# Moving a softmax factor from GpSimd to VectorE, one reciprocal and one product per head

## The reference, cut to what matters

```
q, k, v = x@Wq, x@Wk, x@Wv          # q and k in two halves (q1,q2),(k1,k2), each rotated (rope)
a1 = softmax(q1 k1^T * scale + causal mask);  a2 = softmax(q2 k2^T * scale + causal mask)
lam = exp(sum(lambda_q1*lambda_k1)) - exp(sum(lambda_q2*lambda_k2)) + LAMBDA_INIT
out = (a1 - lam*a2) @ v             # then a norm per head over time, @Wo
x = layernorm(x + attention);  x = layernorm(x + ffn(x))   # silu(up)*gate, ternary weights
```

## Time and profile before

| | us |
|---|---|
| median of 3 runs | 2203.5 (2202.45 to 2203.89) |
| profiled execution, its own time | 2204.31 |
| its span, first to last instruction | 2202.3 |
| TensorE busy in the span | 2124.7 (96%) |
| VectorE busy | 1691.1 (77%) |
| ScalarE busy | 1457.0 (66%) |
| GpSimd busy | 1197.9 (54%) |

### The profile page before, as it was taken

One profiled execution on the slowest core, in us unless ns is written; L12 is line 12 of the kernel. 1 busy time (PEld: TensorE's weight loads), 2 busy tenths in 40 slices (PEclk: granted clock), 3 DMA queues, 4 the chain that ended last, 5 costly groups with the idle time before them and its releaser, 6 DMA issues.

```text
span 2202.3 us, 41179 instructions
## 1 busy us (share of the span) xinstructions
PE 2124.7 (96%) x13314; PEld 1362.0 (62%) x13314; DVE 1691.1 (77%) x3701; ACT 1457.0 (66%) x3450; POOL 1197.9 (54%) x1919
## 2 busy tenths in 40 slices
PE   8999999999999999999999999999999999999998
PEld 4666666666665666666666666666666666654443
DVE  4888787889888878888878888888778888853333
ACT  0777777767777777777767777777677687742232
POOL 0577676677656655555555655655554556541232
PEclk9999999999999999999999999999999999999999
DMA  7766566757656422221453322241543213114000
GB/s 248 202 207 217 194 208 209 239 178 221 191 164 152 136 73 61 89 68 58 150 134 82 94 75 78 91 125 54 166 107 70 71 40 96 40 49 112 4 20 19
DMA packets 291218, 263.85 MB, mean 120 GB/s; under 512 B 65088, under 2 KB 233152, under 8 KB 288960
## 3 DMA queue, kind: packets, MB, share of 16 engines
q1 hardware_dynamic: 246016, 220.26, 33.7%
q10 hardware_dynamic: 44992, 40.98, 6.8%
HBM read 181.48 MB, written 71.30 MB: 115 GB/s over the span
## 4 chain that ended last, share of the span: by engine, by line
PE 76%; DVE 7%; POOL 6%; issue 5%; ACT 4%; DMA 1%; ACTq 1%; DVEq 0%; SPq 0%; POOLq 0%
PE PS L1166 19%; PE PS L1115 10%; PE PS L1096 9%; PE PS L1077 9%; PE PS L1135 9%; PE PS L1175 9%; PE PS L1156 8%; PE PS L1142 2%; POOL linv L1383 2%; DVE e_long L1458 2%; ACT e_long L1227 2%; ACT dt_long L1217 1%; POOL coef L1384 1%; DVE e_long L1524 1%; PE PS L1081 1%
## 5 line engine op out<-in xcount | busy, mean ns | idle before, releaser
L1383 POOL TENSOR_TENSOR linv<-lsum,powers 128x2 f32<-128x2 f32 x512 | 418.3, 817 | 412.5 <-ACT e_long L1227 331.1
L1227 ACT ACTIVATE e_long<-e_long,nmax 128x768 f32<-128x768 f32 (+3 forms) x512 | 504.8, 987 | 150.8 <-DVE nmax L1458 145.1
L1458 DVE CUSTOM_DVE_ANT_0 e_long<-PS,mask_b 128x768 f32<-128x768 f32 (+3 forms) x512 | 516.1, 1019 | 70.6 <-PE PS L1096 49.7
L1096 PE MATMUL PS<-kstk,qstk 128*128 128x384 f32 (+5 forms) x1536 | 470.7, 412 | 27.5 <-DVE nmax L1458 16.8
L1096 PEld LDWEIGHTS PS<-kstk,qstk 128*128 128x128 f32 x1536 | 268.2, 190 | 149.9 <-issue 84.2
L1217 ACT ACTIVATE dt_long<-PS 128x512 f32<-128x512 f32 (+3 forms) x544 | 257.8, 514 | 131.6 <-PE PS L1077 120.8
L1524 DVE SCALAR_TENSOR_TENSOR e_long<-e_long,coef 128x1024 f32<-128x1024 f32 (+3 forms) x256 | 276.3, 1079 | 69.6 <-POOL coef L1384 69.0
L1227 ACT ACTIVATE e_short<-e_short,nmax 128x384 f32<-128x384 f32 (+3 forms) x512 | 283.1, 557 | 17.6 <-DVE nmax L1458 16.8
L1396 POOL TENSOR_TENSOR hid<-th,hid 128x512 f16<-128x512 f32 x128 | 147.9, 1160 | 248.3 <-DVE e_short L1524 124.5
L1077 PE MATMUL PS<-ident,e_long 128*128 128x128 f32 x1664 | 238.8, 275 | 14.8 <-DVE e_long L1524 6.2
L1384 POOL TENSOR_SCALAR coef<-lsum,linv,neglam 128x1 f32<-128x1 f32 x512 | 219.7, 429 | 53.4
(11 more groups left out here) (117 smaller groups left out, 3124.0 us busy)
## 6 DMA issues: line engine op xcount, KB each, us to landing
qstk<-dq SPq DMA_DIRECT2D x512, 128.0 KB, 2.9
dq<-hl SPq DMA_DIRECT2D x25, 1024.0 KB, 5.0
wr<-in_w_proj ACTq DMA_DIRECT2D x48, 512.0 KB, 4.9
kstk<-dk SPq DMA_DIRECT2D x64, 256.0 KB, 5.2
da<-ra SPq DMA_DIRECT2D x32, 512.0 KB, 3.5
at_sb<-da SPq DMA_DIRECT2D x32, 512.0 KB, 4.3
wt<-in_w_up SPq DMA_DIRECT2D x16, 512.0 KB, 6.3
wt<-in_w_gate SPq DMA_DIRECT2D x16, 512.0 KB, 5.4
```

What stands on the lines that cost most here:

```text
L1096: last = nc.tensor.matmul(slot[:, h, :], qstk[:, duo % 4, 2 * r + m, :].bitcast(F32R), kstk[:, g % 2, m, h * w:(h + 1) * w].bitcast(F32R), ...
L1227: nc.scalar.activation(e, e, ACT.Exp, bias=nmax[:, u % 8:u % 8 + 1], scale=-1.0, accum_out=lsum[:, n % 4, m:m + 1]).then_inc(s_exp, 1)
L1383: link(nc.gpsimd.tensor_tensor(linv[:, a % 8, :], lsum[:, a % 4, :], mone, ALU.pow))
L1458: nc.vector.tensor_tensor_reduce(out, slot, mask, -1.0, -NEG, ALU.add, ALU.min, nmax[:, u % 8:u % 8 + 1]).then_inc(s_negmax, 1)
```

## The change: what it does, and the diff

The item "factor" moves from GpSimd's strings to VectorE's. For each head VectorE takes the reciprocal of the second sum (128x1) and then a product of the first sum, that reciprocal and -lambda (128x1), with a link between the two. GpSimd keeps a new item, "inverse", once per duo: a power of -1 on the duo's two first sums (128x2) and the broadcast copy into `wide`. It waits for the exponential of map 0 of the second head only, and is placed before the last `turn` of that head. `lsum` gets 8 places in place of 4, `linv` 4 in place of 8, and `coef` 4 columns in place of 2 (two hold the reciprocals). The planner's cost of "factor" becomes 0.4 in place of 1.15 or 1.4, and "inverse" costs 1.1.

```diff
@@ takes
-    if what == "factor":
-        return 1.4 if STEPS[a].r else 1.15
-            "hidden low": 1.32, "rsqrt": 1.5, ... "group": 1.5, "settle": 1.25, "side": 1.1}
+            "hidden low": 1.32, "rsqrt": 1.5, ... "group": 1.5, "factor": 0.4, "inverse": 1.1, "settle": 1.25, "side": 1.1}
@@ after
     elif what == "turn":
         out = [ITEM("combine", a)]
+        if STEPS[a].r and b == turns(a) - 1:
+            out.append(ITEM("inverse", STEPS[a].duo))
...
     elif what == "factor":
         out = [ITEM("exponent", a, 1), ITEM("minus lambda")]
-        if STEPS[a].r and STEPS[a].duo >= 2:
-            second = heads_of(STEPS[a].duo - 2)[1]
+    elif what == "inverse":
+        out = [ITEM("exponent", heads_of(a)[1], 0)]
+        if a >= 2:
+            second = heads_of(a - 2)[1]
             out.append(ITEM("turn", second, turns(second) - 1))
@@ STRINGS
     "dve": [[ITEM("minimum", n, m) for n, m in _maps],
-            [ITEM("combine", n) for n in _heads], [ITEM("product", duo) for duo in range(DUOS)],
+            [ITEM("factor", n) for n in _heads], [ITEM("combine", n) for n in _heads], [ITEM("product", duo) for duo in range(DUOS)],
...
-    "pool": [[ITEM("factor", n) for n in _heads], [ITEM("hidden low", j) for j in OF_KIND["gate"]],
+    "pool": [[ITEM("inverse", duo) for duo in range(DUOS)], [ITEM("hidden low", j) for j in OF_KIND["gate"]],
@@ tiles
-        lsum = sb("lsum", [P, 4, 2])
-        linv = sb("linv", [P, 8, 2])
-        coef = sb("coef", [P, 2])
+        lsum = sb("lsum", [P, 8, 2])
+        linv = sb("linv", [P, 4, 2])
+        coef = sb("coef", [P, 4])
@@ exponent (ScalarE)
-                                     accum_out=lsum[:, n % 4, m:m + 1]).then_inc(s_exp, 1)
+                                     accum_out=lsum[:, n % 8, m:m + 1]).then_inc(s_exp, 1)
@@ GpSimd
-                if what == "factor":
-                    duo = STEPS[a].duo
-                    pool.wait_ge(s_exp, 2 * a + 2)
-                    link(nc.gpsimd.tensor_tensor(linv[:, a % 8, :], lsum[:, a % 4, :], mone, ALU.pow))
-                    nc.gpsimd.tensor_scalar(coef[:, a % 2:a % 2 + 1], lsum[:, a % 4, 0:1], linv[:, a % 8, 1:2],
-                                            neglam[:, :], ALU.mult, ALU.mult).then_inc(s_coef, 1)
-                    if STEPS[a].r:
-                        if duo >= 2:
-                            second = heads_of(duo - 2)[1]
-                            pool.wait_ge(s_tb, TURN[second, turns(second) - 1] + 1)
-                        nc.gpsimd.tensor_copy(wide[:, duo % 2, :, :], linv[:, (a - 2) % 8:a % 8 + 1:2, 0:1]
-                                              .broadcast_to((P, 2, 64))).then_inc(s_wide, 1)
+                if what == "inverse":
+                    first, second = heads_of(a)
+                    pool.wait_ge(s_exp, 2 * second + 1)
+                    link(nc.gpsimd.tensor_tensor(linv[:, a % 4, :], lsum[:, first % 8:second % 8 + 1:2, 0], mone, ALU.pow))
+                    if a >= 2:
+                        last = heads_of(a - 2)[1]
+                        pool.wait_ge(s_tb, TURN[last, turns(last) - 1] + 1)
+                    nc.gpsimd.tensor_copy(wide[:, a % 2, :, :], linv[:, a % 4, :].rearrange("p (r o) -> p r o", o=1)
+                                          .broadcast_to((P, 2, 64))).then_inc(s_wide, 1)
@@ VectorE
                 if what == "minimum":
                     neg_max(a, b)
+                elif what == "factor":
+                    dve.wait_ge(s_exp, 2 * a + 2)
+                    if a == 0:
+                        dve.wait_ge(s_neglam, 1)
+                    link(nc.vector.reciprocal(coef[:, 2 + a % 2:3 + a % 2], lsum[:, a % 8, 1:2]))
+                    nc.vector.tensor_scalar(coef[:, a % 2:a % 2 + 1], lsum[:, a % 8, 0:1], coef[:, 2 + a % 2:3 + a % 2], neglam[:, :],
+                                            ALU.mult, ALU.mult).then_inc(s_coef, 1)
```

More of the change, by code:

```diff
@@ L261, in takes @@
             "store rotated": 0.45, "store a": 0.45, "store out": 0.5, "load weight": 0.5, "load v": 0.5, "load lambda": 0.8, "lambda sums": 0.5,
-            "hidden low": 1.32, "rsqrt": 1.5, "rotate": 1.35, "low": 1.3, "group": 1.5, "settle": 1.25, "side": 1.1}.get(what, 0.06)
+            "hidden low": 1.32, "rsqrt": 1.5, "rotate": 1.35, "low": 1.3, "group": 1.5, "factor": 0.4, "inverse": 1.1, "settle": 1.25, "side": 1.1}.get(what, 0.06)
 def after(item):
```

## The result

The changed kernel takes 2214.84 us (median of 4 runs, 2212.84 to 2217.69) against 2203.18 (4 runs, 2202.45 to 2203.89): a ratio of 1.0054, 95% interval 1.0041 to 1.0067, that is 11.7 us slower. The forecast was 2227 us. The sign held and the time lies in the range, but the loss is half of the one forecast. The profiled execution took 2212.84 us, its span 2210.7.

What follows compares the result with a forecast made beforehand. The prediction took TensorE as the bound, busy for 2124.7 of 2202.3 us, and VectorE as second limit. It summed 2204.3 + 16 + 15 - 8 = 2227.3, less 0.8 for the median: 2227 us, range 2189 to 2264.

Steps and rivals of the forecast that it cites:

- The pair: VectorE's reciprocal and product for each head: 0.41 us taken, 210 us (169 to 251) for 512 heads.
- The waits for the factor: VectorE's waits before combinations, 97.3 us: the factor comes 0.9 us earlier, so 94.7 us in two stretches go.
- GpSimd lighter: GpSimd does about 430 us less, worth nothing directly; a TensorE wait for a late inverse costed at nothing.
- Meetings: Combinations on VectorE lengthened by running long GpSimd operations: 25 us taken, 15 early and 10 late, bounds 0 and 50.
- the blind case: Combinations falling blindly among long GpSimd operations: 100 of 512 meet one and lose 0.5 us each, 50 us.
- The rival in which meetings decide: All 50 us of lengthened combinations fall on VectorE: 2272 us, range 2250 to 2290, chance 0.13.
- Its variant: A running GpSimd operation holds VectorE's product, in a fifth of cases for 0.5 us: 50 us more of VectorE.
- The stalls that end with a combination, -8: TensorE's stalls ending with a combination that waited for its factor, 6.2 us, and their clock cost go: -8 us.
- Early, +16: 100 to 800 us: 695 us of VectorE work plus a third of 61.5 us of waits, 21, makes 716 in 700.
- Late, +15: 800 to 1940 us: TensorE's idle share rises with VectorE's load, 50 us at full slope; a third taken, +15.
- The two full slopes: TensorE idle time if it rises fully with VectorE's load: early 36 us, in the meetings rival, and late 50 us.
- The rival "nothing moves": Loss and gain cancel, with TensorE's work the same and its order planned anew: 2200 to 2208 us, chance 0.13.

Runs made afterwards that it cites:

- run 13: Changed kernel in its own order, GpSimd's long operations no longer waiting for the combination of the last placed factor: 2248.49 us (1.0210).
- run 3: Kernel before with an idle reciprocal and product on VectorE ahead of each combination, GpSimd still making the factor: 2321.13 us (1.0533).
- run 1: The changed kernel's instructions in the order of the kernel before, each pair right ahead of its combination: 2297.25 us (1.0435).
- run 4: Changed kernel with the pair issued twice for each head, the first one idle: 2402.06 us (1.0908).
- run 5: Changed kernel in its own order, with each pair moved on VectorE to right ahead of its combination: 2258.77 us (1.0251).
- run 14: Changed kernel planned with factor cost 0.5 and ScalarE's measured transfer issue times (2194.91 us), here without GpSimd's long operations waiting for combinations: 2228.67 us (1.0117).
- the crossed runs: Changed instructions in the order of before: 2297.25 us; instructions of before in the changed kernel's order: 2269.16 us.
- three orders made alike: Both kernels planned with the pace of the scores at 3.70, 3.75 and 3.80: changed minus before +31.3, +11.7 and +3.8 us.
- the changed kernel with 0.5: Changed kernel planned with 0.5 in place of 0.4 as the cost of the factor, same instructions: 2201.24 us (0.9993).
- run 10: Changed kernel with one sign moved ahead of ScalarE's transfers and one rounding behind two emptyings on VectorE, near 540 us: 2213.58 us (1.0057).

## Why the prediction was wrong in size

*The pair: right.* 170 slots of 0.50 and 342 of 0.385 make 217 us, forecast 210. Single values were off in ways that cancel: the reciprocal took 156 ns as forecast, the product 273 in place of 210, but another instruction covers its end in 342 of 512 cases. The busy time rose by 160 only, in place of 190 to 250, because it counts the overlap of product and next instruction once.

*The waits for the factor: right in kind, too good in size.* All of 97.3 us went, and the exponential is late next as the prediction said. But it is late by 42.5 us in all, where the prediction left some 10 at most of such waits.

*GpSimd lighter: right.* No TensorE wait for the inverse.

*Meetings: too high.* 22 combinations started within a long operation, not 50, and lost 4.5 us in all, not 25. The placement rule still sets every long operation behind a combination; run 13 shows what lies behind it: without the guard the combinations take 48 us more of VectorE's time, near the 50 of the blind case, at 34 us of the kernel's. The rival in which meetings decide needed one in five lengthened; it was 22 of 512. Its variant, a product that is held, is refuted: 83 of the 512 products started while a long GpSimd operation ran, 56 of them with more than 0.3 us of it left, and all 512 took 272 to 278 ns. The Trainium skill (VectorE: DVE Perf Modes, section "Mode 2×_2P — use both read ports for one tensor") lets a single-source operation use both ports only if its outermost dimension of more than one element is even, or odd and equal in source and destination. A 128x1 product has no such dimension, and the 128x3 one of the earlier trace rows has, so the trace agrees on both. For the combinations the Trainium skill (SBUF — State Buffer, section "Who interferes with whom") has an instruction with two SBUF inputs contend with a GpSimd one that reads SBUF. The trace agrees in kind: the 72 further meetings of run 13 cost 48 us, 0.67 us each.

*The stalls that end with a combination, -8: did not go.* TensorE still waits 7.2 us for combinations in 10 times (7.1 in 6 before). The single one of 2.7 us in the earlier trace rows is gone, others of up to 2.0 stand in its place. In the fixed order the earlier factor together with the lighter GpSimd is worth 24 us (run 3 against run 1), but that is the price of the waits that went as well.

*Early, +16: half.* Put in the measured load (81 us of pairs, about 3 of meetings) and the same working gives 600.7 + 84 + 21 - 700 = +6; measured +7.1. That it comes so near is partly luck, for the third that makes the 21 was chosen.

*Late, +15: the step that failed.* "if all of the slope is VectorE's doing. I take a third." The measured value is -3.4, with the pairs' time near the forecast (307 of them, 130 us in place of 126). In the old order, with the same instructions, the late stretch has 32.4 us more of TensorE's idle time than before (57.3 against 24.9) and the early one 22.2 (58.5 against 36.3). The two full slopes that stand in the prediction, 36 + 50 = 86 us, are near the 94 that the change costs there, but not for their reasons alone: only 58 of it are idle time, 34 are TensorE's own busy time, and the 36 had counted 50 us of meetings, where the old order has one, at no loss. Each unplanned microsecond of VectorE cost 0.66 to 1.07 us: 94/109 (run 1: 206 us of work less 97 of waits), 118/155 (run 3), 187/208 (run 4), 44/41 (run 5), 34/46 (run 13), 34/51 (run 14). What I didn't price was that the order is made anew: I read 1/3 as a share of the engine's doing, where the question was how much a planner that knows the new cost gives back. It gave back 82 of 94 us here: 15 us of idle time early, and 36 late, more than the whole late loss. The sum has no term of this kind. The rival "nothing moves" names the new plan, with a chance of 0.13 and without a price; the crossed runs price it.

*Open.* Whether the remaining 11.7 us are the change's own. The difference is +4 to +31 us in three orders made alike, and the changed kernel with 0.5 is level with before. The scatter from order to order, 39 us for one kernel and 26 for the other, is larger than the effect. The largest single piece, the 6.8 us stall, comes from transfers, sign and rounding that stand together, but run 10 did not remove it, and so did not show it to be the loss. That the places of such stalls make the scatter from order to order is argued, not shown.

*Signs that the prediction named.* Wrong: VectorE over 95% busy early (93.7%), its busy time up by 190 to 250 us (160), waits for minima growing (12.7), the end of attention moving by what the total moves (11 us sooner, with a total 8.4 later). Right: no wait for GpSimd at the combination, its maxima past 1.4 us (2.0), GpSimd near 770 (801).

## What to carry to other kernels

Where the order of every engine is computed before the program is written, price a change twice: once in the old order (here 0.66 to 1.07 us per us of the second limit, though that engine idles for 16 to 23% of the span), and once for what a new plan gives back, and before believing a difference below the scatter of plans (here 1 to 2%) make a few plans of both kernels with an unrelated knob moved. Crossing order and instructions costs two runs and says at once which of the two prices one is looking at. And in this kernel a combination right behind the product that it reads cost VectorE 0.115 us more than another instruction in that place: where there is a choice, put one between.

## What the runs showed of the hardware that I had not expected

- A product on 128x1 with two values per partition takes 273 ns, with one 198 to 215, with constants 140; a reciprocal 156. So the 210 ns taken from the nearest row was 63 short.
- The combination, which waits for the product and reads it, starts 0.50 us after the reciprocal; other instructions start 0.385 us after it. The product's own record is 273 ns in both cases.
- Transfers are not free for the engine that issues them: on ScalarE 0.38 to 0.75 us each in the mean, the transposing ones 1.35 us (32 times), and they come in groups of five to seven that hold it for 2.5 to 4.6 us.
- A combination that starts beside a running long GpSimd operation loses about what is left of it less 0.2 us. In the changed kernel it was 498 ns with 698 left, 736 with 933.
